# Value projection of two head pairs at once, as seven block products in every other visit, in a fused linear-attention kernel on one core

## The reference, cut to what matters

```python
xn = layernorm(x)                       # x: 4 batches, 512 tokens, 512 features
qkv = silu(xn @ w_qkv.T)                # 16 heads of 128: q, k, v
# per head, blocks of 64 tokens with a running state kv:
o   = (q * q_decay) @ kv + ((q @ k.T) * diag_decay) @ v
kv  = block_decay * kv + (k * k_decay).T @ v
out = norm_w * rms_norm(o)              # over all 2048 columns
s   = (sigmoid(xn @ w_gate.T) * out) @ w_out.T
g   = silu(xn * sum(topk_w) + topk_w @ expert_bias[topk])   # router, top 8 of 64
y   = x + s * g
```

## Time and profile before

| what | value |
|---|---|
| median of 3 runs | 1140.15 us (1139.29 to 1141.92) |
| the profiled execution | 1139.64 us, its span 1137.9 us |
| TensorE busy | 1100.3 us, 97% of the span, 6366 matmul records |
| VectorE busy | 844.4 us, 74% |
| ScalarE busy | 610.0 us, 54% |
| GpSimd busy | 107.6 us, 9% |
| mean granted clock of TensorE | 0.992 |

### The profile page before, as it was taken

How to read it: one execution, slowest core, us unless ns; L and a number is a source line. 1 busy time by engine, 2 the same in 40 slices (tenths; PEclk the granted TensorE clock), 3 DMA queues, 4 the chain that set the end, 5 groups by cost and what they waited for, 6 DMA issues and landing times.

```text
span 1137.9 us, 16238 instructions
## 1 busy us (share of the span) xinstructions
PE 1100.3 (97%) x6366; PEld 955.3 (84%) x6366; DVE 844.4 (74%) x1637; ACT 610.0 (54%) x1308; POOL 107.6 (9%) x99
## 2 busy tenths in 40 slices
PE   6999999999999999999799999999999999999997
PEld 5778989888898978889688888888988889898885
DVE  8578787785877778786666887868668787767756
ACT  4466464554646455474436655646555564655542
POOL 4000000000000001101010000000000000000002
PEclk8999999999999999999999999999999999999999
DMA  4522111131211323322112341311212122121403
GB/s 135 165 84 84 42 48 65 56 94 37 66 56 39 94 82 102 103 65 84 37 48 100 104 156 60 101 47 47 75 47 74 29 93 65 43 68 39 139 1 130
DMA packets 37566, 85.46 MB, mean 75 GB/s; under 512 B 4320, under 2 KB 8688, under 8 KB 37488
## 3 DMA queue, kind: packets, MB, share of 16 engines
q1 hardware_dynamic: 37488, 84.41, 23.5%
HBM read 73.88 MB, written 14.71 MB: 78 GB/s over the span
## 4 chain that ended last, share of the span: by engine, by line
PE 78%; DVE 14%; ACT 4%; DMA 2%; issue 1%; POOL 1%; POOLq 0%; DVEq 0%
PE psR L215 46%; PE psB L215 15%; PE psO L215 8%; PE psS L215 7%; DMA raw<-w 1%; PE psS L637 1%; ACT zh L720 1%; DVE gl L386 1%; DVE T L715 1%; DVE xl L298 1%; DVE yacc L776 1%; DVE wvl L386 1%; DVE T L662 1%; ACT ph L664 1%; DVE zl L725 1%
## 5 line engine op out<-in xcount | busy, mean ns | idle before, releaser
L737 POOL TENSOR_TENSOR ss<-ss,sq 128x512 f32<-128x512 f32 x58 | 78.2, 1349 | 836.5 <-ACT sq L721 836.5
L215 PE MATMUL psR<-xh,gh 128*128 128x512 f32 x384 | 127.8, 414 | 0.2
L720 ACT ACTIVATE zh<-T,nw 128x512 fp32r<-128x512 f32 x64 | 46.3, 724 | 139.7 <-DVE T L715 139.7
L215 PE MATMUL psR<-xl,gh 128*128 128x512 f32 x384 | 119.2, 392 | 0.0
L215 PE MATMUL psR<-xh,gl 128*128 128x512 f32 x384 | 118.6, 390 | 0.0
L215 PE MATMUL psR<-woh,zh 128*128 128x512 f32 x250 | 103.5, 414 | 9.9 <-DVE xl L298 5.7
L215 PE MATMUL psR<-woh,zl 128*128 128x512 f32 x250 | 97.8, 391 | 0.0
L215 PE MATMUL psR<-wol,zh 128*128 128x512 f32 x250 | 97.5, 390 | 0.0
L215 PE MATMUL psB<-xh,gh 128*128 128x512 f32 x288 | 92.9, 404 | 4.3 <-ACT psB L513 2.3
L386 DVE TENSOR_TENSOR gl<-raw,gh 128x256 fp32r<-128x256 f32 x144 | 86.1, 598 | 7.3 <-ACT gh L385 4.7
L215 PE MATMUL psR<-wvh,xh 128*128 128x256 f32 x512 | 88.1, 295 | 2.5 <-DVE xl L298 2.4
(11 more groups left out here) (187 smaller groups left out, 2628.9 us busy)
## 6 DMA issues: line engine op xcount, KB each, us to landing
raw<-w SPq DMA_DIRECT2D x80, 512.0 KB, 3.6
D<-dtab SPq DMA_DIRECT2D x32, 256.0 KB, 2.7
xs<-x SPq DMA_DIRECT2D x28, 256.0 KB, 3.0
gscr<-xs SPq DMA_DIRECT2D x16, 256.0 KB, 2.0
xs<-xnorm SPq DMA_DIRECT2D x16, 256.0 KB, 3.5
out_dram<-yacc SPq DMA_DIRECT2D x16, 256.0 KB, 2.0
dtab<-dscr SPq DMA_DIRECT2D x2, 1792.0 KB
xs<-gscr SPq DMA_DIRECT2D x14, 256.0 KB, 4.1
```

The source lines that it names most:

```text
L215: return lambda e: e.matmul(o, l, r, start=start, stop=stop, skip_group_check=shared)
L720: hi = act.do(lambda a: a.activation(zh[:, i, :], T[:, t, :], ACT.Copy, scale=half), z, nw_ev, *zfree)
L737: a = lane.do(lambda g: g.tensor_add(ss[:, j, :], ss[:, j, :], sq[:, :]), q, ss_ev.get(j))
```

## The change

Two visits share their values. `value_blocks(v)` takes the value pieces of visits v and v + 1 (both weight buffers at once) and makes seven block combinations of 512 columns in a ring of three slots: four additions on VectorE, seven copies on ScalarE, seven subtractions on VectorE. `four_heads(v)` makes the values of four heads and two batches in seven products for each token half c: 7 x 2 x 12 matmuls of 256 columns. For c = 1 the second and third accumulator are in `psS`, where otherwise the scores are. The results go to `vf`, which now has a place for the odd and one for the even visit. This is called in the even visits 2 to 14 after the scores of unit 0, once at the start and once in `closing`; odd visits make no values.

What moves with it: `sequence` loads the value pieces of two visits in a row, ahead of the queries' and keys' at the start; `xs` has 4 instead of 6 rows, `T` 4 instead of 5 tiles, `sg` 5 instead of 6; the output of batch 1 of the visit before comes ahead of the mix of unit 0 in odd visits; most hooks of odd visits move into `second_keys` and `gates`; `gates` mixes unit 2 ahead of p4. The code of `heads`, `second_keys` and `gates` is printed below in the diff.

```diff
-NX = 6
-NT = 5
+NX = 4
+NT = 4
+EARLY = (0, 3, 1, 2, 4, 5, 6)
...
-            sequence += [(p, r) for p in (VV, QK0, GG, QK1)]
+            sequence += [(VV, r), (VV, r + 1), (QK0, r), (GG, r), (QK1, r)]
             for v in range(r, r + 7):
-                values_last = [(VV, v + 1)] if v == r else []
-                sequence += [] if values_last else [(VV, v + 1)]
-                sequence += [(GG, v + 1), (QK0, v + 1), (OO, v), (QK1, v + 1)] + values_last
+                sequence += [(GG, v + 1), (QK0, v + 1), (OO, v), (QK1, v + 1)]
+                if v % 2 and v < r + 6:
+                    sequence += [(VV, v + 1), (VV, v + 2)]
...
+        def value_blocks(v, order=(0, 1, 2, 3, 4, 5, 6)):
...
+            def let_first(lo):
+                rring.give(i, lows[3], lo)
+                load_piece()
...
+                if n == 0:
+                    make(0, a11, lda)
+                elif n == 1:
+                    sums[1] = dve.do(lambda v: v.tensor_add(total, a21, a22), ldb, *wt2_free[0])
+                    make(1, total, sums[1])
+                elif n == 2:
+                    sums[2] = dve.do(lambda v: v.tensor_sub(total, total, a11), lda, lows[1])
+                    sums[4] = dve.do(lambda v: v.tensor_sub(a21, a21, a11), ldb, sums[1])
+                    make(2, total, sums[2])
...
+                elif n == 5:
+                    e = dve.do(lambda v: v.tensor_sub(a11, a12, total), lows[0], sums[2], sums[4])
+                    wt2_free[0] = (lows[2], e)
+                    make(5, a11, e, then=let_first)
+                elif n == 6:
+                    make(6, a22, ldb, then=let_second)
...
+        def four_heads(v):
...
+            def product(n, c, dst, start, *after):
+                iw, ix = FACTORS[n]
+                k, lo = v_block[iw]
+                for m in range(2):
...
+                    ops = [(xh[:, ix, q, tk], wvh[:, k, ws[q]]) for q in range(2)]
+                    ops += [(xh[:, ix, q, tk], wvl[:, k, ws[q]]) for q in range(2)]
+                    ops += [(xl[:, ix, q, tk], wvh[:, k, ws[q]]) for q in range(2)]
...
+            def p1(*cs):
+                for c in cs:
+                    settle()
+                    i, free = ring.take()
+                    A[c] = psR[:, i, :], i
+                    ev = product(1, c, A[c][0], True, *free)
+                    B[c] = (psB[:, :], b_free[0]) if c == 0 else (psS[:, 0:512], s_free[0])
+                    seed[c] = act_copy(B[c][0], A[c][0], ev, *B[c][1])
...
         def second_keys(v, nx, early=True, hung=(None, 3)):
...
+            hook(v, hung[0])
             p7()
-            if not early:
-                hook(v, 3)
+            hook(v, hung[1])
...
+        def heads(v, last=False):
             first_keys(v, prep(QK1, v))
+            if v % 2:
+                do_out(v - 1, 0, between({}, lambda: do_mix(v - 1, 3), None, None, None))
+                do_scores(v, 0)
+                split_keys(1)
+                split_queries(1)
+                split_values(v, 0)
+                if not last:
+                    do_out(v - 1, 1, between({}, None, lambda: do_state(v, 0), None, None))
+                    do_mix(v, 0)
+                else:
+                    do_state(v, 0)
+                    do_mix(v, 0)
+                do_scores(v, 1)
+                split_values(v, 1)
+                hook(v, 0)
...
+        def steady(v):
+            heads(v)
+            if v % 2:
+                second_keys(v, prep(GG, v + 1), False, (1, 2))
+                gates(v, prep(QK0, v + 1), out_weights(v), (3, 4))
```

More of the change, by code:

```diff
@@ L234, in row, with take_row, give_row @@
         def row(i):
-            return xs[:, i, :] if i < NX else yacc[:, (i - NX) // 4, (i - NX) % 4, :]
+            if i < NX:
+                return xs[:, i, :]
+            i -= NX
+            if i < 8:
+                return yacc[:, i // 4, i % 4, :]
+            return vf[:, 0, (i - 8) // 2, (i - 8) % 2, :]
+        def take_row(spare):
+            if not spare:
+                return xring.take()
+            i, free = aside.take()
+            return NX + 8 + i, free
+        def give_row(i, *evs):
+            if i < NX:
+                xring.give(i, *evs)
+            else:
+                aside.give(i - NX - 8, *evs)
         def load_early(tt):
@@ L425, in weights, with make @@
             yield
-        v_ready, v_used, o_ready, o_used = {}, [None], [None], [None]
-        def value_weights(v):
-            i, ld = loaded[(VV, v)]
-            def part(n, src, then, *after):
+        o_ready, o_used = [()], [None]
+        def value_blocks(v, order=(0, 1, 2, 3, 4, 5, 6)):
+            i, lda = loaded[(VV, v)]
+            j = ldb = None
+            a11, a12 = raw[:, i, 0:512], raw[:, i, 512:1024]
+            total = wt2[:, :]
+            sums, lows = {}, {}
+            def make(n, src, *after, then=None):
+                k, free = vring.take()
@@ L448, in value_weights @@
[L448 to L456 removed]
+                split_later(wvh[:, k, :], wvl[:, k, :], src, end, *after, *free)
+            def let_first(lo):
+                rring.give(i, lows[3], lo)
+                load_piece()
@@ new lines, in let_second @@
+            def let_second(lo):
+                rring.give(j, lows[4], lo)
+                load_piece()
+            for n in order:
+                settle()
+                if n in (1, 2, 4, 6) and j is None:
+                    j, ldb = loaded[(VV, v + 1)]
+                    a21, a22 = raw[:, j, 0:512], raw[:, j, 512:1024]
+                if n == 0:
[7 more added lines that the diff above has]
+                    make(2, total, sums[2])
+                elif n == 3:
+                    make(3, a12, lda)
+                elif n == 4:
+                    make(4, a21, sums[4])
+                elif n == 5:
[4 more added lines that the diff above has]
+                    make(6, a22, ldb, then=let_second)
+                yield
@@ new lines, in steady, with closing @@
+        def steady(v):
[3 more added lines that the diff above has]
+                gates(v, prep(QK0, v + 1), out_weights(v), (3, 4))
+            else:
+                second_keys(v, prep(GG, v + 1), True, (None, None))
+                gates(v, prep(QK0, v + 1), out_weights(v))
+        def closing(v, fill):
+            heads(v, True)
+            aside.free = [(i, (v_free[(0, 0)], v_free[(0, 1)])) for i, _ in aside.free]
+            second_keys(v, iter(()), False, (1, 2))
+            hook(v, 3)
@@ L1341, in build @@
         spread_decay(1, PAIRS)
+        mingle_first(0)
+        next(blocks)
+        mingle_first(1)
+        place_first(0)
+        next(blocks)
+        place_first(1)
+        mingle_first(2)
+        next(blocks)
+        settle()
+        p5(0)
+        p6(0)
+        place_first(2)
+        mingle_first(3)
+        p7(0)
+        place_first(3)
+        p5(1)
+        next(blocks)
+        p6(1)
+        next(blocks)
+        p7(1)
         qw = weights(QK0, 0)
@@ L1373, in build @@
             steady(v)
-        for k, tt in enumerate(range(8, 14)):
+        for k, tt in enumerate(range(8, 12)):
             later(15, k // 2, lambda tt=tt: fetch_gate(tt))
+            later(15, 2, lambda k=k: fetch_gate_aside(12 + k, k))
         v, before, now = 15, range(8, 12), range(12, 16)
-        heads(v, iter(()), True)
+        heads(v, True)
+        hook(v, 1)
+        hook(v, 2)
         for t in range(4):
             weigh(0, t, 8 + t)
-        second_keys(v, iter(()))
-        fetch_gate_aside(14, 0)
-        fetch_gate_aside(15, 1)
+        second_keys(v, iter(()), False)
         ow = out_weights(v)
```

343 lines of the change are left out of this document (189 added, 154 removed).

## The result

The change makes the kernel slower: 1192.76 us median of 3 runs (1192.14 to 1193.37) against 1140.15, a ratio of 1.0459 with a 95% interval of 1.0435 to 1.0482. The forecast was 1147 us in a range of 1134 to 1158. The sign was right, the size was not: 52.6 us where 7 were expected.

A forecast was written before the change was run, and what follows sets the result against it. TensorE was taken to bound the middle with the others hidden, and what precedes its matmuls the start. -23 + 15 + 8 + 7 = +7 on 1139.6 gave 1146.6, about 1147 us against the median, range 1134 to 1158.

The forecast's parts named there:

- Matmuls saved, -23.0: All value products: 192 fewer matmuls at 0.120 us each, all on the path, -23.0 us.
- The start, +15: Start: first p1 waits for QK0 behind the decay table copy; 13.4 us idle, 1.5 half clock; bounds 6 and 17.
- the lower bound: Start, if QK0 doesn't wait: p2's seeds behind four normalisations still delay it, 5 us idle and 1 us of clock.
- Rival (c): Start: QK0 does not wait for the table copy, +6 for +15, 1138 us, no change; chance 0.08.
- Visits 7 and 15, +8: Mix of unit 0 in visits 7 and 15: TensorE waits 3.9 us each for pl and vl, behind kl and ql.
- the bound of 2 us: Visits 7 and 15: 2 us of wait each if VectorE's subtractions came in the best order.
- Odd visits, +7: Odd visits 1 to 5 and 9 to 13: seed waits 5, VectorE 5, less 3 of present waits; bounds 0 and 16.
- VectorE between the mixes: Odd visits, mixes of units 1 to 2: VectorE has slightly too much work, 9.8 us over six visits, half taken, 5.
- Rival (b): Odd visits: VectorE becomes the bound, holding only 80% between mixes 1 and 2; 18 for 7, about 1158 us; chance 0.18.
- Even visits, nothing: Even visits: VectorE's extra value work, some 4.8 us a pair of visits, is hidden by TensorE's longer time; no cost.
- Four rows in `xs` suffice: Token row buffer: four places are enough since the hooks hold three at most; no cost.
- Rival (a): Odd visits, 7 and 15: elementwise engines keep up, seed and pl in time; sum -5, about 1135 us, faster; chance 0.24.

The follow-up runs named there:

- experiment 4: Changed kernel, in second keys of odd visits, 0 and 8 VectorE's addition behind p7 put ahead of hooks, low value parts and a weights step: 1183.95 us, 1.0376.
- experiment 9: Kernel before, in visits 1, 3, 5, 9, 11, 13 value halves put together ahead of the scores, hooks crowded as in the changed kernel: 1176.87 us, 1.0322.
- experiment 12: Changed kernel with table copy later, p7's sum first, visits 7 and 15 reordered, tiles spread, hook 0 early in visit 2, seeds before normalisations: 1159.18 us.

## Why the prediction was right and wrong

- **Matmuls saved, -23.0: right.** 6174 matmuls stand in the page, and two value matmuls still start 0.24 us after the two before.
- **The start, +15: right in size (12.6), partly by luck, and half right in its cause.** I had 13.4 us of idle time and 1.5 of half clock; they grew by 8.8 and 5.6, and the two errors cancel. The landing (61.50 us, had 61.87) and p1 came as forecast. But I had put QK0's issue at 44 to 49 us; its buffer came free only at 51.8, so it took 9.7 us and not 17. And the term that I had kept for the lower bound only, ScalarE's seeds behind four normalisations, was worth as much (7.3 us by the medians, 5.8 at the mix of unit 0) as the copy (6.1 and 6.5).
- **Rival (c), QK0 doesn't wait: wrong.** It took 9.7 us from issue to first use with the copy ahead and 3.5 without it. The Trainium skill (DMA: Bandwidth & Descriptors, Queues, rings and completion order) says that completion is not first in, first out per issuing engine, by which it could have overtaken. It didn't. The trace's packet records show the copy's 3584 packets of 1024 bytes starting until 59.89 us and those of the weights, 4096 bytes each, from 53.57 us: the two shared the DMA engines, and QK0 landed at 61.48 us, behind the copy's last packet.
- **Visits 7 and 15, +8: right in mechanism, 5.8 us too small.** 3.38 us and not 3.9 each, and the best order saved what the bound of 2 us had said (1.61). The rest is mostly half clock, which I had not counted: 6.4 us more than before in these two visits, in three places of visit 7 (from 565.5, 589.4 and 603.1 us) and one of visit 15. TensorE's idle time there grew by only 4.9 us, since other waits shrank; 2.5 us of the 13.8 stand in neither sum. With the order mended the waits are 3.5 us less and 4.7 us of half clock are gone. But visit 7 also has 3.4 to 3.5 us less of it in the profiles of the later table copy and of the spread tiles, where nothing in visit 7 was changed. So how much of that gain is the order's isn't shown.
- **Odd visits, +7: this step failed; it was 30.5.** The seed's wait is there (1.05, 0.39, 0.38 us in visits 1, 3 and 11, none in the others), 1.8 us in all where I had 5. The step that failed is "VectorE between the mixes". I added up durations and compared 20 us of work with 20.2 us of time, as if only the sum mattered. The sums came out: between the mixes of units 1 and 2 of visit 3 TensorE is busy 19.98 us and VectorE 18.21. But the stretch takes 22.92 us, with the wait of 2.94 us in it. VectorE (the fourth number, behind the length, TensorE and its weight loads) is busy 71% of that stretch in visit 11, 83% in visit 1, and 74% of the whole visit 11:

```profile
875.48:898.56 23.08, 20.13 (x95) 16.57 (x94) 16.45 (x32) 13.00 (x29) 1.38 (x1) 0.93 0.11 35
152.05:174.19 22.14, 19.94 (x101) 16.58 (x100) 18.39 (x38) 13.54 (x30) 1.38 (x1) 1.00 0.08 25
853.77:915.90 62.13, 58.80 (x302) 49.55 (x301) 46.16 (x88) 34.09 (x76) 5.51 (x4) 0.97 0.20 60
```

Rival (b) had priced a VectorE that holds only 80% there at 3 us a visit. The share is about that, the loss is 5.1 a visit, and the same operations in another order (experiment 4) took 7.3 us less, so fullness alone doesn't explain it. What decided was which operation stands behind which: the sum of p7, `whl` and kv came 1 to 4.4 us after TensorE wanted them, and nothing was left there to hide it. I never asked, for the moved hooks, who waits for each result; experiment 9 shows that order and missing cover alone make a loss of this size. In the changed kernel itself only 9.1 of the 30.5 us were taken back by order and tiles (the best version, experiment 12); that the other 21.4 have the same cause is argued from experiment 9.
- **Even visits, nothing: this step failed; it was 18.7.** Waits of over 1 us there were what I had named as proof against it, and there are 2.76, 1.47 and 1.70 us. "Four rows in `xs` suffice" was about places, not about time: the row for visit 2 was loaded one product ahead of its use. With it early in visit 2 the visit is 4.2 us shorter, which is shown; in visit 4 the wait of 1.47 us went too, but another of 2.50 came. Without the router 13.5 us remain: 3.8 in visit 2, 2.7 in 4, 4.7 in 8, and 0.7 to 0.8 each in 10, 12 and 14. For visit 8 I have waits (kt 1.24, seed 1.13, T 1.13, ql 1.62 us), of which the seed's stood there before. Experiment 4 took the one for T away, and the one for ql grew to 2.40. What makes the rest of the even visits' loss stays open. More places for rows or tiles of T were not tried.
- **Rival (a), the others keep up: wrong** from the same step. It hung on the seed and on pl, and neither would have helped the sum of p7.
- **The clock was missing from every term but one.** 22.5 us of the loss are half clock. I had counted 1.5.

## What to carry to other kernels

Work that a change saves may have been the cover of something else. Before matmuls are moved out of a stretch, list for each product left there which operand is made last, by which engine, and what stands ahead of it in that engine's order. Comparing sums of busy time with the time at hand doesn't do it: an engine busy 71% of a stretch made another wait 2.95 us in it (visit 11). And where TensorE falls to half its clock at a wait, waits cost about half as much again (22.5 on 45.6 us here). That is an average: the same wait came with and without it.

## What the runs showed of the hardware

**Half the clock around waits of some microseconds, not around each.** In the kernel before the granted clock is full from 41 us until TensorE's work has ended (1133 us). In the changed one it is 0.50 (1.2 of 2.4 GHz) from 443 to 449 us: it falls while TensorE is in the wait of 4.38 us that ends at 444.96, and stays low behind it. The wait for kv is 1.95 us in visit 1 and in visit 9. Behind the first the clock stays at 1.00, behind the second it is down to 0.50 from 760 to 763 us:

```profile
174.00:178.00 4.00, 4.00 (x18) 3.35 (x19) 3.13 (x6) 2.64 (x6) 0.53 (x1) 1.00 0.00 0
760.00:763.00 3.00, 3.00 (x9) 2.38 (x8) 2.17 (x4) 1.64 (x4) 0.04 (x1) 0.51 0.00 0
```

**A GpSimd addition holds up some VectorE operations.** The row at 436.96 us above took 1.39 us where its form takes 0.42. GpSimd had begun 0.26 us earlier:

```profile
436.70 1.36 POOL L858 TENSOR_TENSOR ss<-ss,sq 128x512 f32<-128x512 f32 x1 [6.63 <-ACT sq L842]
```

22 subtractions `vl<-vf,vh` begin in such an addition in the changed kernel and 14 before, all with 1.39 to 1.41 us. Both inputs of `vl` are in SBUF. Operations with one input in PSUM, begun 0.1 to 0.9 us behind the start of one (`T<-psS,D`, `psR<-psB,T`), keep their 0.68 to 0.70 us. In the kernel before, eight operations on token rows were held up too. They have one tensor as input, in SBUF, and take 0.49 to 0.55 us elsewhere:

```profile
179.25 1.52 DVE L276 TENSOR_SCALAR xs<-xs,mv,rstd 128x512 f32<-128x512 f32 x1
```

The Trainium skill (SBUF — State Buffer, Who interferes with whom) says that a VectorE instruction with two SBUF inputs contends with a GpSimd instruction that reads SBUF, and that one with at most one SBUF input does not, outside the modes that use two ports, which `tensor_scalar` can enter. The trace agrees for the subtractions, and the eight rows would be that exception. The change hardly adds to this cost. Summed over the VectorE operations that overlap a GpSimd one, against the median of the same operations elsewhere, it is 27.5 us before and 28.5 after: `vl` loses 8 us more, and the eight row operations, which lost 8 us before, lose nothing. Some of it stands in front of the sum T; no run took it away.
